# Four relus per step of the mixing stage handed from ScalarE to VectorE

## The chip, the core and the metric

The kernel runs on one core of one Trainium2 chip. The metric is the device time of one execution in microseconds; the time before is the median of three runs. The engines of the core, as the profile names them: PE is TensorE's matmuls and PEld its weight loads, DVE is VectorE, ACT is ScalarE, POOL is GpSimd, SP issues most DMAs. Each engine works through its own queue in order, and waits for others by semaphores.

## The reference

A block in three parts: three state-space layers, a complex diagonal recurrence over a layer norm, and a mixture of 32 experts of which each token takes one.

```python
def reference(x, ...):
    h = _L0_tok_ref(x, ...)                       # three state-space layers, halved twice in length
    h = h + _L0_attn_ref(_layernorm(h), ...)      # B u, scan with Lambda_bar, C x, + D u
    h = h + _L0_ffn_ref(_layernorm(h), ...)

def _L0_ffn_ref(x, router_w, router_b, W1, b1, W2, b2):   # E = 32 experts, H = 16 hidden
    logits = xf @ router_w.T + router_b
    idx = jnp.argmax(logits, axis=-1)
    h = jax.nn.relu(jnp.einsum('nd,ndh->nh', xf, W1[idx]) + b1[idx])
    out = jax.nn.relu(jnp.einsum('nh,nhd->nd', h, W2[idx]) + b2[idx])
```

The input is 128 x 375 x 64, the result 128 x 93 x 64. The hidden layer of all experts is 32 x 16 = 512 rows, four tiles of 128; the tokens' unchosen experts are pushed to -1e30 before the relu, so that they come out as zero.

## The kernel before

The first 5.8 ms are the three layers. VectorE scans there (L930), GpSimd multiplies the inputs (L1137), ScalarE takes the exponentials (L716). The change doesn't touch them.

The mixing stage does the other two parts for 16 chunks of 372 columns. Rows are 128: 64 channels of two batches, so every chunk is two halves, b = 0 and b = 1. `mix_steps` runs 20 steps, i = 0 to 19: two and two written out, ten in a hardware loop (steps 4 to 13), six written out. In step i five chunks are in work, a stage apart, and each engine's `step` names them: a = i is normed and driven into the recurrence, y = i - 1 is scanned and brought out, b = i - 2 is normed again and routed, e = i - 3 goes through the experts, f = i - 4 is finished and stored. So step 3 is the first with e, step 4 the first with f; the last with a is step 15, with y 16, with b 17, with e 18.

Per engine, in the order of a step:
- PE: center for a and b (L553); `up` for expert tile k=0 of e (L611 and L617, into the banks `bank_h[0]`, which is in decay, and `bank_h[1]`, which is z_bank); the variances (L553); `open_o` (L553, into prep_bank, the expert output's accumulator); `down` k=0 (L631) and `up` k=1; `output` for y (L553, four instructions with u as operand); `drive` for a; `route` for b; `up` k=2; `open_y`; `down` k=1; `up` k=3; `down` k=2; `turn` (L601, transposes of the choice); `down` k=3. The four `up` of a chunk share one pair of banks, so each waits until the one before has been read.
- ACT: `copy_cold` (L872, L873), squares (L862), `rectify` k=0, the two inverse deviations (L866, L868), `rectify` k=1 to 3. A `rectify` is two relus with bias (L880), one per half, out of `bank_h[b]` into `hid[k % 2][b]`.
- DVE: `scans` (L1085, L1087), `turn_back` (L1093, L1094), `finish` of f (L1100), `scale` for a and b (L1042), the addition of y's output (L1046), four `products` for a (L1053), `pick` for b (L1069 to L1079).
- POOL: `turn` of y (L1153, L1154, then the sums L1159 and L1162, which need DVE's turn_back), `turn_drive` of a (L1168, L1170).

`hid`, `u` and `hT` are one storage for the profile: a relu reads as hT<-decay,u or hT<-z_bank,u. The semaphores that matter: B["hid"] counts up's tiles, B["relu"] the relus read by `up` and `down`, B["down"] frees `hid`, A["qdve"] hands turn_back to POOL, A["turned"] hands POOL's sums to `output`. `open_o` of chunk e waits for B["fin"] of the chunk before it, which is f of the same step, since both use prep_bank:

```python
            def open_o(c):
                pe.wait_ge(B["copied"], 2 * c + 2)
                if not known_below(c, 1):
                    pe.wait_ge(B["fin"], c)
```

Of the kernel before, what the change touches and what calls it, by code (L numbers as in the profile page):

```python
# [6 lines left out]
ALU = mybir.AluOpType  # L7
ACT = mybir.ActivationFunctionType
# [33 lines left out]
TILES = E_FFN // EXP_PER_TILE  # L42
# [11 lines left out]
def known_below(n, limit):  # L54

    return isinstance(n, int) and n < limit


def tower(nc, io, hs, out_dram, n_batch):
# [13 lines left out]
    with ctx:  # L73
# [6 lines left out]
        def sem(name):  # L80
            return ctx.enter_context(nc.semaphore(name))
# [62 lines left out]
        ones_row, b1, eps = u[1][0:1, 1600:1728], u[1][:, 1728:1728 + TILES], u[1][:, 1740:1741]  # L144
        q = [u[2][:, i * W0:(i + 1) * W0] for i in range(4)]
        re, nim = [u[2][:, i * W0:(i + 1) * W0] for i in (4, 5)]
        fin, hot = u[2][:, 6 * W0:7 * W0], u[2][:, 7 * W0:8 * W0]
# [7 lines left out]
        hid = [[hT[1][:, (2 * i + b) * W0:(2 * i + b + 1) * W0] for b in range(2)] for i in range(2)]  # L155
# [5 lines left out]
        bank_h = [db[2][:, BANK:BANK + W0], zb[:, 0:W0]]  # L161
# [14 lines left out]
        m_set = sem("m_consts_set")  # L176
        A = {n: sem("A_" + n) for n in ("xc", "sq", "var", "log", "rstd", "u", "bu", "du", "prod", "w", "z", "qpool", "qdve", "turned", "y", "h")}
        B = {n: sem("B_" + n) for n in ("xc", "sq", "var", "log", "rstd", "u", "logits", "pick", "coldT", "copied",
                                        "hid", "relu", "down", "fin", "out")}
        N_WEIGHTS, N_SMALL = 15, 2  # L180

        def chunk(c):
            return h3[:, bass.ds(c * W0, W0)]

        def stage(i, lag):

            if isinstance(i, int) and not 0 <= i - lag < chunks:
                return None
            return i - lag
# [193 lines left out]
        def _(pe):  # L383
# [221 lines left out]
            def up(half, c, k):  # L605

                if k or not known_below(c, 1):
                    pe.wait_ge(B["relu"], 2 * (TILES * c + k))
                for b in range(2):
                    at = slice(D * b, D * (b + 1))  # L610
                    nc.tensor.matmul(bank_h[b], w1[at, P * k:P * (k + 1)], uB[half][at, :],  # L611
                                     start=True, stop=False, tile_position=(D * b, 0))
                if k == 0:
                    pe.wait_ge(B["copied"], 2 * c + 2)
                for b in range(2):
                    at = slice(D * b, D * b + E_FFN)
                    last = nc.tensor.matmul(bank_h[b], expand[at, k, :], coldT[at, :],  # L617
                                            start=False, stop=True, tile_position=(D * b, 0))
                last.then_inc(B["hid"], 1)
# [6 lines left out]

            def down(c, k):

                pe.wait_ge(B["relu"], 2 * (TILES * c + k + 1))
                for b in range(2):  # L630
                    last = nc.tensor.matmul(bank_o[D * b:D * (b + 1), :], w2[:, D * k:D * (k + 1)], hid[k % 2][b],  # L631
                                            start=False, stop=(k == TILES - 1), tile_position=(0, D * b))
                last.then_inc(B["down"], 1)

            def step(half, i):
# [6 lines left out]
                if e is not None:  # L642
                    up(other, e, 0)
# [46 lines left out]
        def _(act):  # L690
# [184 lines left out]
            def rectify(c, k):  # L875
                act.wait_ge(B["hid"], TILES * c + k + 1)
                if k >= 2 or not known_below(c, 1):
                    act.wait_ge(B["down"], TILES * c + k - 1)
                for b in range(2):
                    nc.scalar.activation(hid[k % 2][b], bank_h[b], ACT.Relu, bias=b1[:, k:k + 1]).then_inc(B["relu"], 1)  # L880

            def step(half, i):
                a, _, b, e = [stage(i, lag) for lag in range(4)]
# [29 lines left out]
        def _(dve):  # L913
# [44 lines left out]
            ts, stt = nc.vector.tensor_scalar, nc.vector.scalar_tensor_tensor  # L958
# [70 lines left out]
            def seqs(t):  # L1029
                return t.rearrange("p (s t) -> p s t", s=SEQS)  # L1030

            def every(t):
                return t.unsqueeze(1).broadcast_to([P, SEQS, T3])

            def scale(s, c, xc, rs, out):
                dve.wait_ge(s["rstd"], c + 1)
                if s is A:
                    if not known_below(c, 1):
                        dve.wait_ge(A["du"], c)
                elif not known_below(c, 2):  # L1040
                    dve.wait_ge(B["hid"], TILES * (c - 1))
                tt(out, xc, rs, ALU.mult).then_inc(s["u"], 1)  # L1042

            def add_output(c):
                dve.wait_ge(A["y"], c + 1)
                tt(chunk(c), chunk(c), bank_y, ALU.add).then_inc(A["h"], 1)  # L1046

            def products(c):
                dve.wait_ge(A["bu"], c + 1)
                if not known_below(c, 1):  # L1050
                    dve.wait_ge(A["w"], 2 * c)
                for i, (bank, table) in enumerate(((bank_v, T1R), (bank_x, T1I), (bank_v, T1I), (bank_x, T1R))):
                    tt(seqs(pr[i]), seqs(bank), every(table), ALU.mult).then_inc(A["prod"], 1)  # L1053

            def pick(c):

                dve.wait_ge(B["logits"], c + 1)
                if not known_below(c, 1):
                    dve.wait_ge(B["coldT"], c)
                shape = [TOK, 2 * NTOK, E_FFN]  # L1060

                def e3(t):
                    return t[0:TOK, 0:2 * NTOK * E_FFN].rearrange("p (j e) -> p j e", e=E_FFN)

                def over(t):
                    return t[0:TOK, :].unsqueeze(2).broadcast_to(shape)

                n = 5 * c
                nc.vector.reduce_max(top[0:TOK, :], e3(bank_xb), mybir.AxisListType.X).then_inc(B["pick"], 1)  # L1069
                dve.wait_ge(B["pick"], n + 1)  # L1070
                tt(e3(eq), e3(bank_xb), over(top), ALU.is_equal).then_inc(B["pick"], 1)
                dve.wait_ge(B["pick"], n + 2)
                tt(score[0:TOK, :], eq[0:TOK, :], rev[0:TOK, :], ALU.mult).then_inc(B["pick"], 1)
                dve.wait_ge(B["pick"], n + 3)
                nc.vector.reduce_max(top2[0:TOK, :], e3(score), mybir.AxisListType.X).then_inc(B["pick"], 1)
                dve.wait_ge(B["pick"], n + 4)

                cold = cold_rows[0:TOK, :].rearrange("p (j e) -> p j e", e=D)[:, :, 0:E_FFN]
                tt(cold, e3(score), over(top2), ALU.not_equal).then_inc(B["pick"], 1)  # L1079

            def scans(c):
                if not known_below(c, 1):
                    dve.wait_ge(A["qpool"], 2 * c)
                dve.wait_ge(A["w"], 2 * c + 1)
                nc.vector.tensor_tensor_scan(zr, DEC, wr, 0.0, ALU.mult, ALU.add).then_inc(A["z"], 1)  # L1085
                dve.wait_ge(A["w"], 2 * c + 2)
                nc.vector.tensor_tensor_scan(zi, DEC, wi, 0.0, ALU.mult, ALU.add).then_inc(A["z"], 1)  # L1087

            def turn_back(c):
                dve.wait_ge(A["z"], 2 * c + 2)  # L1090
                if not known_below(c, 1):
                    dve.wait_ge(A["turned"], 2 * c)
                tt(seqs(q[2]), seqs(zi), every(NSIN), ALU.mult).then_inc(A["qdve"], 1)  # L1093
                tt(seqs(q[3]), seqs(zi), every(COS), ALU.mult).then_inc(A["qdve"], 1)  # L1094

            def finish(c):
                dve.wait_ge(B["down"], TILES * c + TILES)
                if not known_below(c, 1):
                    dve.wait_ge(B["out"], 16 * c)
                stt(fin, bank_o, 0.0, chunk(c), ALU.max, ALU.add).then_inc(B["fin"], 1)  # L1100

            def step(half, i):
                a, y, b, _, f = [stage(i, lag) for lag in range(5)]
                if y is not None:
                    scans(y)
                    turn_back(y)
                if f is not None:
                    finish(f)
                if a is not None:
                    scale(A, a, bank_x, rsA, uA)  # L1110
                if b is not None:
                    scale(B, b, bank_xb[:, 0:W0], rsB, uB[half])
                if y is not None:
                    add_output(y)
                if a is not None:
                    products(a)
                if b is not None:
                    pick(b)

            dve.wait_ge(m_load, 16 * N_WEIGHTS)  # L1120
            mix_steps(dve, FIRST_STEPS, step)
# [139 lines left out]
def build(nc, io, out_dram, n_batch):  # L1261
    pairs = n_batch // 2
    hs = [nc.dram_tensor(f"h_after{l}", (P, pairs * LENGTHS[min(l + 1, LAYERS - 1)]), FP32, kind="Internal").ap()
          for l in range(LAYERS)]
    tower(nc, io, hs, out_dram, n_batch)
# [15 lines left out]
```

## Time and profile before

| | before |
|---|---|
| median of 3 runs | 6117.61 us (6111.73 to 6119.73) |
| profiled execution, its time | 6110.93 us |
| profiled execution, its span | 6109.1 us |
| mean granted TensorE clock | 0.983 |
| busy over the span: PE, DVE, ACT, POOL | 77%, 97%, 82%, 96% |

The span runs from the first instruction to the last; the profiled execution's time has 1.8 us around it. The shares are those of the layers, which fill 95% of the span. The mixing stage is seen in a stretch of its own: steps 4 to 15 run from 5875.05 to 6070.24 us. The columns of a stretch are, after its two ends, its length, then for PE, PEld, DVE, ACT and POOL the busy us and the count of instructions, then the granted clock as a share of full speed, the DMA share and GB/s. In a timeline, "x4" is a merged group of four, and the bracket gives how long the engine sat idle before it and who released it. A matmul's length is modelled and overlaps the next one's start; two `up` matmuls side by side run at once in halves of the array.

### The profile page before, as it was taken

Reading aid. Unit: us, or ns where it says so; the run is one execution under the profiler, and the core shown is the slowest. Engines: PE = TensorE matmul, PEld = TensorE weight load, DVE = VectorE, ACT = ScalarE, POOL = GpSimd, SP = SyncE. Lnnn points to the kernel's source line nnn. Section 1 sums busy time; section 2 is a strip of 40 time slices with the busy share of each in tenths; the row PEclk is TensorE's granted clock in tenths of the full one; section 3 lists DMA queues with packets and bytes.
Section 4 is the critical chain, followed back from the end, with each engine's and each line's share of the span. In section 5 each row is a group of like instructions: output and inputs, shape, how many; then the busy total and the mean of one; then the engine's idle time right before and its main releaser. Section 6 shows DMA issues by size and latency. Waiting matters only on the chain.

```text
span 6109.1 us, 97254 instructions
## 1 busy us (share of the span) xinstructions
PE 4718.7 (77%) x36042; PEld 1952.1 (32%) x36042; DVE 5950.6 (97%) x4016; ACT 5013.3 (82%) x10247; POOL 5888.7 (96%) x996
## 2 busy tenths in 40 slices
PE   6777777777777777777777777777777777777789
PEld 2333333333333333333333333333333333333234
DVE  8999999999999999999999999999999999999965
ACT  7888888888888888888888888888888888888844
POOL 8999999999999999999999999999999999999943
PEclk9999999999999999999999999999999999999999
DMA  7888888888888888888888888888888888888710
GB/s 256 270 269 270 268 269 269 269 269 269 268 268 269 265 272 269 268 270 268 265 267 268 271 269 267 268 269 269 269 270 269 269 269 270 270 270 271 259 42 14
DMA packets 562034, 1565.40 MB, mean 256 GB/s; under 512 B 172129, under 2 KB 320546, under 8 KB 561442
## 3 DMA queue, kind: packets, MB, share of 16 engines
q1 hardware_dynamic: 561570, 1559.30, 78.5%
q8 instruction: 281, 4.60, 0.3%
q14 instruction: 183, 1.50, 0.1%
HBM read 1468.37 MB, written 90.59 MB: 255 GB/s over the span
## 4 chain that ended last, share of the span: by engine, by line
DVE 45%; POOL 44%; issue 6%; PE 5%; ACT 0%; DMA 0%; SPq 0%; ACTq 0%; DVEq 0%; POOLq 0%
DVE hT L930 45%; POOL u L1137 44%; PE decay L553 2%; PE decay L611 1%; PE prep_bank L631 1%; DVE dx L941 0%; PE z_bank L418 0%; PE decay L617 0%; PE decay L400 0%; PE prep_bank L553 0%; PE prep_bank L506 0%; PE decay L601 0%; DMA u<-dx_rows 0%; ACT hT L880 0%; DVE hT L1053 0%
## 5 line engine op out<-in xcount | busy, mean ns | idle before, releaser
L1137 POOL TENSOR_TENSOR u<-u,Bt 128x2976 f32<-128x2976 f32 x896 | 5781.5, 6511 | 28.0 <-DMA u<-dx_rows 27.9
L930 DVE TENSOR_TENSOR_SCAN hT<-decay,u 128x744 f32<-128x744 f32 x3584 | 5740.5, 1681 | 17.4 <-POOL u L1137 12.5
L716 ACT ACTIVATE decay<-decay,a_neg 128x371 f32<-128x371 f32 (+2 forms) x7168 | 3604.1, 545 | 585.6 <-PE decay L400 555.5
L400 PE MATMUL decay<-stk,spread 96*128 96x371 bf16 (+2 forms) x7168 | 1788.4, 332 | 1353.9 <-DVE hT L930 1211.5
L418 PE MATMUL z_bank<-hT,Cst 128*32 128x256 f32 x21472 | 1468.5, 392 | 0.3 <-ACT z_sb L725 0.3
L400 PEld LDWEIGHTS decay<-stk,spread 96*128 96x128 bf16 x7168 | 416.2, 98 | 2852.2 <-DVE hT L930 2678.9
L725 ACT COPY z_sb<-z_bank 128x512 f32<-128x512 f32 x1342 | 790.9, 589 | 259.7 <-PE z_bank L418 259.5
L418 PEld LDWEIGHTS z_bank<-hT,Cst 128*32 128x32 f32 x21472 | 568.1, 111 | 672.3 <-issue 447.0
L428 PE MATMUL z_bank<-stk,spread 96*128 96x372 bf16 x1677 | 355.9, 321 | 0.0
L506 PE MATMUL prep_bank<-tmap,yT 64*128 64x32 f32 (+3 forms) x1344 | 215.3, 281 | 0.6 <-DMA yT<-y_rows 0.6
L506 PEld LDWEIGHTS prep_bank<-tmap,yT 64*128 64x128 f32 x1344 | 177.3, 190 | 110.5 <-issue 109.2
L428 PEld LDWEIGHTS z_bank<-stk,spread 96*128 96x128 bf16 x1677 | 163.4, 97 | 103.3 <-issue 1.1
L479 PE MATMUL prep_bank<-delta,eye 128*128 128x372 f32 x448 | 186.0, 497 | 2.2 <-DVE dx L941 1.7
L1168 POOL TENSOR_TENSOR hT<-hT 128x372 f32<-128x372 f32 x16 | 15.5, 971 | 126.4 <-DVE hT L1053 126.4
L754 ACT ACTIVATE Cst<-prep_bank,own_batch 128x384 f32<-128x384 f32 x224 | 132.3, 591 | 0.0
L880 ACT ACTIVATE hT<-decay,u 128x372 f32<-128x372 f32 x64 | 36.5, 570 | 110.6 <-PE z_bank L617 110.6
L451 PE MATMUL prep_bank<-xT,w_dt_rows 128*128 128x372 f32 x224 | 90.9, 487 | 9.1 <-DMA eye<-in_ident 6.5
L481 PE MATMUL prep_bank<-parts,neg_eye 128*128 128x372 bf16 x336 | 92.2, 329 | 0.0
L778 ACT COPY delta<-prep_bank 128x372 f32<-128x372 f32 x112 | 52.5, 469 | 47.3 <-PE prep_bank L469 47.3
L461 PE MATMUL prep_bank<-t_w,eye 128*128 128x372 f32 x224 | 89.7, 482 | 1.8 <-ACT t_w L763 1.8
L464 PE MATMUL prep_bank<-t_one,eye 128*128 128x372 f32 x224 | 89.7, 481 | 0.0
L468 PE MATMUL prep_bank<-t_ln,eye 128*128 128x372 f32 x224 | 89.5, 481 | 0.0
(140 smaller groups left out, 2533.7 us busy)
## 6 DMA issues: line engine op xcount, KB each, us to landing
u<-dx_rows SPq DMA_DIRECT2D x3584, 372.0 KB, 4.3
delta_parts<-parts SPq DMA_DIRECT2D x112, 279.0 KB, 6.5
stk<-delta_parts SPq DMA_DIRECT2D x112, 279.0 KB, 5.6
y_rows<-z_sb SPq DMA_DIRECT2D x1792, 12.0 KB
yT<-y_rows SPq DMA_DIRECT2D x112, 192.0 KB, 4.6
dx_rows<-dx SPq DMA_DIRECT2D x112, 186.0 KB, 2.8
xT<-in_x SPq DMA_DIRECT2D x64, 186.0 KB, 4.7
xP<-in_x SPq DMA_DIRECT2D x64, 186.0 KB, 4.7
```

The lines of the kernel that those rows point to most:

```text
L400: nc.tensor.matmul(slot[:, e, :, 1:], spread[0:PARTS * QR, TILES_G * q + er // TILES_G, :], src[:, er % TILES_G, :, 1:], start=True, stop= ...
L418: last = nc.tensor.matmul(bank[TB * 2 * g:TB * 2 * (g + 1), kk * EPT * TB:(kk + 1) * EPT * TB], Cst[buf][:, CG * (2 * i + kk) + g, :, :], ...
L428: nc.tensor.matmul(zb[:, 0:W0], spread[0:PARTS * QR, 0, :], stk[buf][0:PARTS * QR, 0, :], start=True, stop=True)
L479: nc.tensor.matmul(prep[:, 0:W0], eye[:, :], delta[:, :], start=True, stop=False)
L481: last = nc.tensor.matmul(prep[:, 0:W0], neg_eye[:, :], parts[:, j, :], start=False, stop=(j == i))
L506: last = nc.tensor.matmul(prep[:, k * w:k * w + m], yT[:, k, :], tmap[:, base:base + m], start=False, stop=(k == KB - 1))
L553: return nc.tensor.matmul(dst, wt, src, start=start, stop=stop)
L716: last = nc.scalar.activation(bank, bank, ACT.Exp, scale=a_neg[:, l, c:c + 1])
L725: nc.scalar.copy(z_sb[buf][:, 2 * i:2 * i + 2, :, q * EPT:(q + 1) * EPT], src).then_inc(s_zev, 1)
L754: ins = nc.scalar.activation(Cst[buf][:, :, b, :], prep[:, 0:COLS_Z].rearrange("p (k t) -> p k t", t=TB), ACT.Identity, scale=own[:, b:b + 1])
L930: nc.vector.tensor_tensor_scan(hT[q % 2][:, i * PAIR:(i + 1) * PAIR], pair_slot(turn, p), u[c % RING][:, part * PAIR:(part + 1) * PAIR], 0 ...
L1137: tt(here, here, Bt[buf][:, :].unsqueeze(1).broadcast_to([P, 2 * HALVES * CHUNK, W0]), ALU.mult).then_inc(s_u, 1)
```

## The change

A new `rectify` in VectorE's queue takes the half b = 1: one tensor_scalar, add the bias and take the maximum with zero, from `bank_h[1]` into `hid[k % 2][1]`. It waits for the same B["hid"] and B["down"] as ScalarE's, and counts a semaphore of its own, B["reluv"]. ScalarE's `rectify` keeps the half b = 0. `up` and `down` wait for both counts. In VectorE's step the four calls stand behind the scans (k=0), behind the scales (k=1), behind the products (k=2) and behind pick (k=3).

```diff
--- before.py
+++ after.py
@@ -176,7 +176,7 @@
         m_set = sem("m_consts_set")
         A = {n: sem("A_" + n) for n in ("xc", "sq", "var", "log", "rstd", "u", "bu", "du", "prod", "w", "z", "qpool", "qdve", "turned", "y", "h")}
         B = {n: sem("B_" + n) for n in ("xc", "sq", "var", "log", "rstd", "u", "logits", "pick", "coldT", "copied",
-                                        "hid", "relu", "down", "fin", "out")}
+                                        "hid", "relu", "reluv", "down", "fin", "out")}
         N_WEIGHTS, N_SMALL = 15, 2
 
         def chunk(c):
@@ -605,7 +605,8 @@
             def up(half, c, k):
 
                 if k or not known_below(c, 1):
-                    pe.wait_ge(B["relu"], 2 * (TILES * c + k))
+                    pe.wait_ge(B["relu"], TILES * c + k)
+                    pe.wait_ge(B["reluv"], TILES * c + k)
                 for b in range(2):
                     at = slice(D * b, D * (b + 1))
                     nc.tensor.matmul(bank_h[b], w1[at, P * k:P * (k + 1)], uB[half][at, :],
@@ -626,7 +627,8 @@
 
             def down(c, k):
 
-                pe.wait_ge(B["relu"], 2 * (TILES * c + k + 1))
+                pe.wait_ge(B["relu"], TILES * c + k + 1)
+                pe.wait_ge(B["reluv"], TILES * c + k + 1)
                 for b in range(2):
                     last = nc.tensor.matmul(bank_o[D * b:D * (b + 1), :], w2[:, D * k:D * (k + 1)], hid[k % 2][b],
                                             start=False, stop=(k == TILES - 1), tile_position=(0, D * b))
@@ -876,8 +878,7 @@
                 act.wait_ge(B["hid"], TILES * c + k + 1)
                 if k >= 2 or not known_below(c, 1):
                     act.wait_ge(B["down"], TILES * c + k - 1)
-                for b in range(2):
-                    nc.scalar.activation(hid[k % 2][b], bank_h[b], ACT.Relu, bias=b1[:, k:k + 1]).then_inc(B["relu"], 1)
+                nc.scalar.activation(hid[k % 2][0], bank_h[0], ACT.Relu, bias=b1[:, k:k + 1]).then_inc(B["relu"], 1)
 
             def step(half, i):
                 a, _, b, e = [stage(i, lag) for lag in range(4)]
@@ -1093,6 +1094,13 @@
                 tt(seqs(q[2]), seqs(zi), every(NSIN), ALU.mult).then_inc(A["qdve"], 1)
                 tt(seqs(q[3]), seqs(zi), every(COS), ALU.mult).then_inc(A["qdve"], 1)
 
+            def rectify(c, k):
+
+                dve.wait_ge(B["hid"], TILES * c + k + 1)
+                if k >= 2 or not known_below(c, 1):
+                    dve.wait_ge(B["down"], TILES * c + k - 1)
+                ts(hid[k % 2][1], bank_h[1], b1[:, k:k + 1], 0.0, ALU.add, ALU.max).then_inc(B["reluv"], 1)
+
             def finish(c):
                 dve.wait_ge(B["down"], TILES * c + TILES)
                 if not known_below(c, 1):
@@ -1100,9 +1108,12 @@
                 stt(fin, bank_o, 0.0, chunk(c), ALU.max, ALU.add).then_inc(B["fin"], 1)
 
             def step(half, i):
-                a, y, b, _, f = [stage(i, lag) for lag in range(5)]
+                a, y, b, e, f = [stage(i, lag) for lag in range(5)]
                 if y is not None:
                     scans(y)
+                if e is not None:
+                    rectify(e, 0)
+                if y is not None:
                     turn_back(y)
                 if f is not None:
                     finish(f)
@@ -1110,12 +1121,18 @@
                     scale(A, a, bank_x, rsA, uA)
                 if b is not None:
                     scale(B, b, bank_xb[:, 0:W0], rsB, uB[half])
+                if e is not None:
+                    rectify(e, 1)
                 if y is not None:
                     add_output(y)
                 if a is not None:
                     products(a)
+                if e is not None:
+                    rectify(e, 2)
                 if b is not None:
                     pick(b)
+                if e is not None:
+                    rectify(e, 3)
 
             dve.wait_ge(m_load, 16 * N_WEIGHTS)
             mix_steps(dve, FIRST_STEPS, step)
```

VectorE's queue at the opening of a step, here step 14, the first behind the loop. Before: scans, turn_back, finish, the scales.

```order
L1085 SCALAR_TENSOR_TENSOR hT<-tables,hT 128x372 [waits A_w,A_qpool]
L1087 SCALAR_TENSOR_TENSOR hT<-tables,hT 128x372 [waits A_w]
L1093 TENSOR_TENSOR u<-hT,tables 128x372 [waits A_turned,A_z]
L1094 TENSOR_TENSOR u<-hT,tables 128x372
L1100 SCALAR_TENSOR_TENSOR u<-prep_bank,z_sb 128x372 [waits B_out,B_down]
L1042 TENSOR_TENSOR hT<-decay,hT 128x372 [waits A_du,A_rstd]
L1042 TENSOR_TENSOR hT<-decay,hT 128x372 [waits B_hid,B_rstd]
```

After, from the scans to the relu of k=1 (z_bank is `bank_h[1]`):

```order
L1086 SCALAR_TENSOR_TENSOR hT<-tables,hT 128x372 [waits A_w,A_qpool]
L1088 SCALAR_TENSOR_TENSOR hT<-tables,hT 128x372 [waits A_w]
L1102 TENSOR_SCALAR hT<-z_bank,u 128x372 [waits B_down,B_hid]
L1094 TENSOR_TENSOR u<-hT,tables 128x372 [waits A_turned,A_z]
L1095 TENSOR_TENSOR u<-hT,tables 128x372
L1108 SCALAR_TENSOR_TENSOR u<-prep_bank,z_sb 128x372 [waits B_out,B_down]
L1043 TENSOR_TENSOR hT<-decay,hT 128x372 [waits A_du,A_rstd]
L1043 TENSOR_TENSOR hT<-decay,hT 128x372 [waits B_hid,B_rstd]
L1102 TENSOR_SCALAR hT<-z_bank,u 128x372 [waits B_down,B_hid]
```

The relu of k=0, which waits for TensorE's tile of this step, now stands ahead of turn_back and of finish.

ScalarE's queue in the same step, from the first square on, before:

```order
L862 ACTIVATE hT<-decay 128x372 [waits A_xc]
L862 ACTIVATE hT<-decay 128x372 [waits B_xc]
L880 ACTIVATE hT<-decay,u 128x372 [waits B_down,B_hid]
L880 ACTIVATE hT<-z_bank,u 128x372
L866 ACTIVATE hT<-decay,u 128x372 [waits A_var]
L868 ACTIVATE hT<-hT 128x372 [waits A_log]
L866 ACTIVATE hT<-decay,u 128x372 [waits B_var]
L868 ACTIVATE hT<-hT 128x372 [waits B_log]
L880 ACTIVATE hT<-decay,u 128x372 [waits B_down,B_hid]
L880 ACTIVATE hT<-z_bank,u 128x372
```

After:

```order
L864 ACTIVATE hT<-decay 128x372 [waits A_xc]
L864 ACTIVATE hT<-decay 128x372 [waits B_xc]
L881 ACTIVATE hT<-decay,u 128x372 [waits B_down,B_hid]
L868 ACTIVATE hT<-decay,u 128x372 [waits A_var]
L870 ACTIVATE hT<-hT 128x372 [waits A_log]
L868 ACTIVATE hT<-decay,u 128x372 [waits B_var]
L870 ACTIVATE hT<-hT 128x372 [waits B_log]
L881 ACTIVATE hT<-decay,u 128x372 [waits B_down,B_hid] x3
```

Each pair of relus has become one; its waits are the same.

## Rows read from the trace of the kernel before

**Rows 1.** Busy time by stretch, steps 4 to 15; columns as in the line of engines above.

```profile
5875.05:6070.24 195.19, 195.19 (x853) 85.97 (x853) 118.56 (x205) 94.58 (x193) 80.28 (x73) 1.00 0.03 12
```

**Rows 2.** Timeline, opening of one steady step; start, length, engine, line, instruction, operands.

```profile
5971.57 1.07 DVE L1093 TENSOR_TENSOR u<-hT,tables 128x372 f32<-128x372 f32 x1
...
5972.56 1.25 DVE L1094 TENSOR_TENSOR u<-hT,tables 128x372 f32<-128x372 f32 x1
...
5973.74 0.53 DVE L1100 SCALAR_TENSOR_TENSOR u<-prep_bank,z_sb 128x372 f32<-128x372 f32 x1
...
5974.61 0.96 POOL L1162 TENSOR_TENSOR u<-u 128x372 f32<-128x372 f32 x1
...
5975.30 0.57 ACT L880 ACTIVATE hT<-decay,u 128x372 f32<-128x372 f32 x1 [0.69 <-PE z_bank L617]
...
5976.46 0.79 PE L553 MATMUL prep_bank<-u 128*128 128x372 f32 x2
...
5979.05 1.52 PE L553 MATMUL decay<-u 128*128 128x372 f32 x4
```

**Rows 3.** Timeline, end of the step before that one, all engines.

```profile
5967.49 0.35 DVE L1069 TENSOR_REDUCE u<-decay 124x6 f32<-124x192 f32 x1
...
5967.98 0.57 ACT L880 ACTIVATE hT<-decay,u 128x372 f32<-128x372 f32 x1 [4.06 <-PE z_bank L617]
...
5969.29 0.36 DVE L1079 TENSOR_TENSOR u<-u 124x192 f32<-124x192 f32 x1
...
5970.67 0.57 ACT L880 ACTIVATE hT<-decay,u 128x372 f32<-128x372 f32 x1 [1.65 <-PE z_bank L617]
...
5971.33 0.54 PE L601 MATMUL decay<-eye,u 124*128 124x124 f32 x3
...
5971.80 0.85 PE L631 MATMUL prep_bank<-hT,u 128*64 128x372 f32 x4
```

**Rows 4.** Timeline, VectorE instructions from which prices are taken.

```profile
21.35 0.41 DVE L1020 TENSOR_SCALAR tables<-tables,z_sb 128x368 f32<-128x368 f32 x1
...
5965.67 1.90 DVE L1053 TENSOR_TENSOR hT<-decay,tables 128x372 f32<-128x372 f32 x4 [0.69 <-PE decay L553]
...
5968.27 0.60 DVE L1073 TENSOR_TENSOR u<-u 124x192 f32<-124x192 f32 x1
...
6079.04 0.36 DVE L1073 TENSOR_TENSOR u<-u 124x192 f32<-124x192 f32 x1
```

**Rows 5.** Timeline, steps 16 to 18, TensorE and ScalarE.

```profile
6072.20 0.57 ACT L880 ACTIVATE hT<-decay,u 128x372 f32<-128x372 f32 x1 [0.61 <-PE z_bank L617]
...
6072.81 0.79 PE L553 MATMUL prep_bank<-u 128*128 128x372 f32 x2
...
6080.43 0.58 PE L611 MATMUL decay<-hT,u 64*128 64x372 f32 x1 [0.35 <-ACT hT L880]
...
6096.44 0.89 PE L553 MATMUL prep_bank<-u 128*128 128x372 f32 x2
...
6096.55 0.57 ACT L880 ACTIVATE hT<-decay,u 128x372 f32<-128x372 f32 x1 [1.02 <-PE z_bank L617]
...
6097.02 0.56 ACT L880 ACTIVATE hT<-z_bank,u 128x372 f32<-128x372 f32 x1
...
6097.63 0.84 PE L631 MATMUL prep_bank<-hT,u 128*64 128x372 f32 x4 [0.30 <-ACT hT L880]
...
6100.69 0.58 PE L611 MATMUL decay<-hT,u 64*128 64x372 f32 x1 [1.12 <-ACT hT L880]
```

**Rows 6.** Timeline and busy time by stretch, TensorE in steps 2 and 3.

```profile
5849.94 1.52 PE L553 MATMUL decay<-u 128*128 128x372 f32 x4 [1.75 <-POOL u L1162]
...
5856.84 0.54 PE L601 MATMUL decay<-eye,u 124*128 124x124 f32 x3 [2.14 <-DVE u L1079]
5857.21 2.22 PE L553 MATMUL decay<-z_sb,u 128*128 128x372 f32 x4
...
5858.00:5860.00 2.00, 2.00 (x5) 0.83 (x5) 1.97 (x3) 1.19 (x3) 2.00 (x2) 0.50 0.00 0
```

## The prediction

> **What bounds the kernel now.** I read the slices of the span first, then the granted clock, then the mixing stage alone. The change touches only that stage: twenty steps behind the last scan of the three state-space layers, about the last 290 of 6109 us. In busy time by stretch, TensorE is busy for all of the 195.19 us of steps 4 to 15, at the full granted clock [rows 1]; that is 16.27 us a step. VectorE has work for 118.56 us of them and ScalarE for 94.58 us. So what ends last in a steady step is TensorE's own queue, and no engine that gets rid of work there gives time back. A step can only grow, if TensorE is made to wait. Only in the last three steps, where few chunks are left in flight, does TensorE wait for ScalarE's two relus [rows 5].
>
> So the question is which VectorE results TensorE needs, and when. I put the timeline of one steady step next to VectorE's order of work. VectorE runs ahead: it turns the chunk back (L1093, L1094) at 5971.57 and 5972.56, finishes the oldest chunk (L1100) at 5973.74, and is done with that at 5974.27, while the first hidden tile of this step is there only at 5975.30, when ScalarE's first relu starts [rows 2]. TensorE opens the output bank (L553, prep_bank) at 5976.46; open_o waits for this very finish, because the bank still holds the oldest chunk. The slack is 2.2 us.
>
> **Part by part.** *ScalarE loses one relu of two, four times a step.* In steps 4 to 15 this is worth nothing: TensorE has no gap behind it [rows 1].
>
> *VectorE gains four instructions a step*, some 2.2 us on 9.9 of 16.27 us: no bound as a sum. What matters is the place. The first one (k=0) stands between the scans and turn_back, and VectorE takes its queue in order. Behind it are queued: both turn_back products (GpSimd waits for them, and TensorE's output for GpSimd), then finish (TensorE's open_o waits for it, and behind open_o all the rest of the step). In the order before, none of these waited for the hidden tile; now all do. The walk, from the hidden tile at 5975.30 [rows 2]:
> - relu, then the first product 0.50 later. Four PSUM-read products in a row take 1.90 us, the last 0.54 of it, so 0.45 from start to start [rows 4]; I add 0.05 for the column of biases.
> - first product to second 0.50. It is 0.99 in the trace [rows 2], but there GpSimd works beside it. Now GpSimd has long done its own two products when VectorE comes, and sits waiting. A product with both operands in SBUF takes 0.60 beside GpSimd and 0.36 alone [rows 4]; so I take the uncontended pace, 0.50, with 0.99 as the upper end.
> - second product to finish 1.10. In the trace it is 1.18 [rows 2]. GpSimd's sum is released by the first product, so it again runs beside the second one. Lower end 0.50, if it did not matter.
> - finish 0.53 [rows 2], hand-over to TensorE 0.05 (a relu that starts at 6097.02 and lasts 0.56 releases a matmul at 6097.63 [rows 5]).
>
> That is 2.68 us: open_o at 5977.98 and not at 5976.46, **1.52 us later per step**. TensorE idles for it, and everything behind it moves along. Twelve steps: 18.2 us. In step 3 there is no finish, so it is free of this.
>
> *The other three relus* I cost at nothing, and name the cover. k=1 runs between scale and the output's addition, where VectorE idles anyway. k=2 is put ahead of pick. Pick starts at 5967.49 but the hidden tile is there only at 5967.98; so it waits 0.49 and then takes 0.50 for the relu, and ends at 5970.65 plus 0.05 instead of 5969.65. TensorE's transposes of its result start at 5971.33 [rows 3]: 0.6 us are left. k=3 comes behind it, at its hidden tile of 5970.67, and ends at about 5971.25, and TensorE's use of it is at 5971.80 [rows 3]. This slack moves along with the step.
>
> *A rule weighed.* The relu reads PSUM. The one instruction of its kind and width in the trace reads SBUF and takes 0.41 [rows 4], while reads from PSUM with the same columns go at 0.54. I take the PSUM price. The Trainium skill, VectorE: DVE Perf Modes, section Why PSUM operands drop a tier, says that fp32 with a PSUM operand stays at the plain rate, which speaks for the same. With 0.41's pace each step would lose 1.4 us, and the sum would be some 2 us lower.
>
> *The two added waits of TensorE* (reluv beside relu) sit on the same matmul instruction; the instruction count of its queue is the same, and I cost them at nothing.
>
> *Last steps.* Step 16 still has turn_back, but no new chunk, so open_o stood only 0.61 behind the hidden tile [rows 5]: 2.68 - 0.61 = 2.07 later; the relu gap of 0.35 [rows 5] goes: +1.7. Step 17 has only finish behind the relu: 0.50 + 0.53 + 0.05 = 1.08, less the same 0.61, +0.47; its gap of 0.35 (as at 6080.43) goes: +0.1. Step 18: hidden tile at 6096.55, so open_o at 6097.63 and not 6096.44, but its down had waited until 6097.63 for the second relu, and now follows 0.72 after open_o, at 6098.35: +0.7. Behind it the gap of 1.12 shrinks by the 0.47 between the two relus' starts, and two gaps of 0.35 go: -1.2. Together -0.5.
>
> **Sum:** 18.2 + 1.7 + 0.1 - 0.5 = +19.6 us on the profiled execution of 6110.93, so 6130.5. The median of the runs shown is 6117.61, so the forecast is **6137.2 us**, 0.32% slower. About 0.2%, 12 us, is what a measurement can tell from no change here.
>
> **Rivals.**
> - *The port is free (ends on the other side).* If turn_back's second product goes at 0.50 too, open_o is late by 0.92 a step: 12 x 0.92 + 1.1 + 0.1 - 0.5 = +11.7, 6129.3, within 0.2%. It decides at 0.54 for that product's pace. For: the shares of contention are read from one row pair. Against: 1.25 us for this very instruction when GpSimd runs [rows 2], and the sum on GpSimd is released just as it starts. Chance 0.12.
> - *The clock falls.* An idle TensorE may get the low clock. After 1.75 us of idle the four matmuls took 1.52; after 2.14 us four took 2.22, at a granted clock of 0.50, that is 1.2 GHz [rows 6]. My 1.52 us lies below the first. If it falls in every step, it adds 0.70 for four matmuls, and I estimate twice that, 1.4, for the whole stretch: 12 x 1.4 = 17, 6154. It is at hand if the first product too is held up (0.99): then the idle is 2.0 and the sum without any clock effect +26. Chance 0.14 for both, from 6143 to 6157.
> - *The finish is not what binds.* If open_o had another cover, the next that is late would be the output's wait for GpSimd's last sum: it ended at 5975.57 against 5979.05 [rows 2], and the walk puts it at about 5978.3. Then only the last steps' gaps count, some -2 us: 6115.5. Against: the wait is in the code, and nothing else holds finish back. Chance 0.06.
> - *More waits in a chain.* If pick ends over 0.6 us later than I say, the transposes and with them the end of every step come late; each 0.1 us over it costs 1.2 us. Chance 0.05.
>
> **How the numbers follow.** Forecast 0.63. Range: from the free port to the fallen clock, 6127 to 6157; what is left out is the case that nothing binds and half of the long chain, under 0.1, plus the scatter of the runs. Slower by over 0.2%: the forecast, the clock and the chain, 0.81. Within 0.2%: free port and no binding, less a little, 0.17. Faster by over 0.2% would need 12 us, and the gaps behind relus hold under 3 us in all: 0.02.
>
> **What would show it.** Right: in steps 4 to 15 a step takes about 17.8 us; TensorE has one idle of about 1.5 us before open_o, released by VectorE's finish; VectorE's longest wait is for the hidden tile, between the scans and turn_back; the first product of turn_back is short (about 0.55) and the second long (over 1). The last step is shorter. Wrong: steps of 16.3 us; an idle ahead of the transposes or the output instead; a granted clock under 1.00 in these steps.

## The result: 14 us slower, and the profile after

| | before | changed |
|---|---|---|
| median of 20 runs | 6113.14 us (6107.73 to 6119.73) | 6127.59 us (6120.2 to 6131.05) |
| ratio, 95% interval | | 1.0024 (1.0018 to 1.003) |
| profiled execution, span | 6109.1 us | 6123.7 us |

The change costs 14.5 us by the medians, 0.24%. The forecast was 6137.2, +19.6 us on a median of 6117.61 from three runs; over twenty runs the kernel before has 6113.14. So of the 9.6 us between forecast and result, 4.5 are the base and 5.1 are the cost.

The two profiled spans differ by 14.6 us. By stretch, with the columns as ahead of the prediction; first the changed kernel, steps 4 to 15 and the rest of the span behind them:

```profile
5875.72:6083.25 207.53, 198.08 (x855) 84.88 (x853) 127.12 (x253) 73.89 (x145) 75.80 (x73) 1.00 0.03 11
6083.25:6123.70 40.45, 33.49 (x162) 12.65 (x160) 15.26 (x32) 11.88 (x23) 4.02 (x4) 1.00 0.05 19
```

and the same two stretches of the kernel before:

```profile
5874.97:6070.17 195.20, 195.20 (x854) 85.97 (x852) 118.58 (x205) 94.59 (x193) 80.29 (x73) 1.00 0.03 12
6070.17:6109.10 38.93, 33.10 (x162) 12.66 (x160) 8.29 (x18) 17.17 (x35) 2.76 (x3) 1.00 0.06 20
```

The twelve steady steps take 207.53 us instead of 195.20, +12.3, and the last three with what follows +1.5. The remaining 0.7 us up to the span's 14.6 lie ahead of step 4: the layers ended 3.7 us earlier in this execution and steps 0 to 3 took 4.5 us longer. That part does not follow the edit, as the nine traces show below under "Steps 0 to 3". In the steady stretch TensorE is no longer busy throughout: 198.08 of 207.53 us.

Timeline of one steady step's opening in the changed kernel, all engines (it corresponds to [rows 2]; L1102 is VectorE's relu, L1108 finish):

```profile
5962.26 1.52 PE L553 MATMUL decay<-z_sb,u 128*128 x4
...
5964.99 0.57 ACT L881 ACTIVATE hT<-decay,u 128x372 f32<-128x372 f32 x1 [0.69 <-PE z_bank L618]
5965.00 0.60 DVE L1102 TENSOR_SCALAR hT<-z_bank,u 128x372 f32<-128x372 f32 x1 [2.38 <-PE z_bank L618]
5965.52 0.54 DVE L1094 TENSOR_TENSOR u<-hT,tables 128x372 f32<-128x372 f32 x1
...
5965.98 0.54 DVE L1095 TENSOR_TENSOR u<-hT,tables 128x372 f32<-128x372 f32 x1
5966.19 1.17 POOL L1176 TENSOR_TENSOR u<-u 128x372 f32<-128x372 f32 x1 [1.99 <-DVE u L1094]
...
5966.44 0.54 DVE L1108 SCALAR_TENSOR_TENSOR u<-prep_bank,z_sb 128x372 f32<-128x372 f32 x1
...
5967.12 0.86 PE L553 MATMUL prep_bank<-u 128*128 128x372 f32 x2 [0.80 <-DVE u L1108]
...
5967.32 0.97 POOL L1179 TENSOR_TENSOR u<-u 128x372 f32<-128x372 f32 x1
...
5979.57 1.52 PE L553 MATMUL decay<-z_sb,u 128*128 x4
```

VectorE stands idle for 2.38 us ahead of the relu of k=0, with turn_back and finish queued behind it. Then relu, two products and finish run in one go, and TensorE's open_o is released by finish, after 0.80 us of idle. From the hidden tile (5964.99) to open_o it is 2.13 us; in the kernel before 1.16 [rows 2]. The step is 17.31 us instead of 16.27.

### The profile page after: what moved, and what is told of

It reads as the page before. It is cut to its first block, busy times and chain, and to the rows that moved or that the text cites. A ratio compares the mean times of both kernels' runs of the same rounds, so it can differ in the third digit from the quotient of the medians.

```text
span 6123.7 us, 97478 instructions
## 1 busy us (share of the span) xinstructions
PE 4705.0 (77%) x36042; PEld 1942.5 (32%) x36042; DVE 5967.1 (97%) x4080; ACT 4995.7 (82%) x10183; POOL 5883.6 (96%) x996
## 4 chain that ended last, share of the span: by engine, by line
POOL 88%; issue 7%; PE 4%; DVE 1%; DMA 0%; SPq 0%; ACT 0%; DVEq 0%; POOLq 0%; ACTq 0%
POOL u L1154 88%; PE decay L553 2%; PE decay L612 1%; PE prep_bank L633 1%; PE decay L618 0%; PE prep_bank L553 0%; DVE hT L931 0%; PE decay L601 0%; DVE u L1108 0%; DMA u<-dx_rows 0%; DVE u L1095 0%; DVE u L1094 0%; DVE hT L1054 0%; DVE hT L1086 0%; POOL u L1170 0%
## 5 line engine op out<-in xcount | busy, mean ns | idle before, releaser
L1102 DVE TENSOR_SCALAR hT<-z_bank,u 128x372 f32<-128x372 f32 x64 | 38.7, 605 | 79.4 <-PE z_bank L618 79.4
```

## The experiments

The base of every edit is the changed kernel. Lengths of steps are from start to start of the centering matmuls (L553, decay<-z_sb).

**Finish ahead of the relu.**

```diff
                 if y is not None:
                     scans(y)
+                if f is not None:
+                    finish(f)
                 if e is not None:
                     rectify(e, 0)
                 if y is not None:
                     turn_back(y)
-                if f is not None:
-                    finish(f)
```

> The changed kernel with one swap in VectorE's step: finish stands ahead of the relu of k=0, turn_back behind it. Theory (the whole cost is finish held back by the wait for the hidden tile): open_o finds its bank free, steps 4 to 15 take 16.27 us again, TensorE has no idle before open_o; GpSimd's last sum comes about 3.3 us behind the hidden tile and TensorE's output 3.75 behind it, so that turn_back's delay stays hidden. Against the kernel before: 0 to -2 us, ratio 0.9997 to 1.0000. Rival 1 (turn_back's delay counts too): an idle ahead of the output, steps of 16.5 to 17 us, +3 to +9 us. Rival 2 (it is VectorE's extra load, or the second wait on TensorE's matmuls): steps stay at 17.3 us, ratio 1.002.

Measured: 6114.19 us, ratio 0.9999 (0.999 to 1.0009), as the theory has it and neither rival. Steps 4 to 15 and the rest, by stretch:

```profile
5880.38:6075.58 195.20, 195.20 (x854) 85.85 (x852) 128.50 (x253) 73.91 (x145) 75.84 (x73) 1.00 0.03 12
6075.58:6112.60 37.02, 33.10 (x162) 12.85 (x160) 15.45 (x32) 11.87 (x23) 4.02 (x4) 1.00 0.06 21
```

VectorE has a little more to do than in the changed kernel (128.50 us), TensorE's matmuls still wait for two semaphores, and the twelve steps are back at 195.20. So neither the load nor the second wait costs anything. And turn_back, which still stands behind the relu, is hidden, with little to spare; the timeline of one step:

```profile
5980.73 0.60 DVE L1102 TENSOR_SCALAR hT<-z_bank,u 128x372 f32<-128x372 f32 x1 [1.88 <-PE z_bank L618]
...
5981.87 0.79 PE L553 MATMUL prep_bank<-u 128*128 128x372 f32 x2
...
5983.05 0.97 POOL L1179 TENSOR_TENSOR u<-u 128x372 f32<-128x372 f32 x1
...
5984.45 1.52 PE L553 MATMUL decay<-u 128*128 128x372 f32 x4
```

GpSimd's last sum ends at 5984.02 and TensorE's output starts at 5984.45, unhindered: 0.43 us are left. The last steps are 1.9 us shorter than before the change (37.02 against 38.93). That is the change's whole gain. It is read from one trace of each kernel, and too small to be seen in the comparison of runs.

**Relu behind turn_back and finish.**

```diff
-                if e is not None:
-                    rectify(e, 0)
                 if y is not None:
                     turn_back(y)
                 if f is not None:
                     finish(f)
+                if e is not None:
+                    rectify(e, 0)
```

> The changed kernel with the relu of k=0 behind turn_back and finish instead of ahead of them; all four relus stay on VectorE. Theory: nothing that TensorE or GpSimd needs is queued behind the hidden tile any more; steps 4 to 15 take 16.27 us, the last three steps are some 2 us shorter than before. Ratio to the kernel before 0.9995 to 1.0000. Rival (load or second wait): steps of 17.3 us, ratio 1.002.

Measured: 6113.69 us, ratio 1.0 (0.9991 to 1.0009).

```profile
5878.42:6073.62 195.20, 195.20 (x855) 85.86 (x853) 142.95 (x253) 73.91 (x145) 80.31 (x73) 1.00 0.03 12
6073.62:6111.20 37.58, 33.26 (x162) 12.77 (x160) 16.70 (x32) 11.87 (x23) 4.40 (x4) 1.00 0.06 21
```

All four relus are on VectorE, which is now busy for 142.95 us, more than in any other of these kernels, and nothing is lost. A surprise is that figure: the same 253 instructions take 14.5 us more than with finish alone moved. The timeline shows where: turn_back meets GpSimd's products again, as it did before the change.

```profile
5976.42 1.07 DVE L1094 TENSOR_TENSOR u<-hT,tables 128x372 f32<-128x372 f32 x1
5977.05 1.21 POOL L1171 TENSOR_TENSOR u<-hT,tables 128x372 f32<-128x372 f32 x1
5977.41 1.25 DVE L1095 TENSOR_TENSOR u<-hT,tables 128x372 f32<-128x372 f32 x1
```

**Only k=0 given back to ScalarE**, and **only k=0 on VectorE.** KS stands here for the tuple that says which relus of the half b = 1 are VectorE's: (1, 2, 3) in the first kernel, (0,) in the second. The counts that TensorE waits for in `up` and `down` follow from it and are left out here. The first piece of the diff is ScalarE's rectify, the second VectorE's.

```diff
             def rectify(c, k):
...
-                nc.scalar.activation(hid[k % 2][0], bank_h[0], ACT.Relu, bias=b1[:, k:k + 1]).then_inc(B["relu"], 1)
+                for b in range(1 if k in KS else 2):
+                    nc.scalar.activation(hid[k % 2][b], bank_h[b], ACT.Relu, bias=b1[:, k:k + 1]).then_inc(B["relu"], 1)
...
             def rectify(c, k):
+                if k not in KS:
+                    return
```

> Of the change only k=1, 2 and 3 are left on VectorE; both relus of k=0 are ScalarE's again. Theory: steps of 16.27 us, the last steps about 1.5 us shorter, ratio 0.9996 to 1.0000. Rival (each of the four relus bears its share): three quarters of the cost stay, +10 us, steps of 17.0 us.

Measured: 6113.94 us, ratio 0.9998 (0.9989 to 1.0007).

> Of the change only k=0 is on VectorE, still ahead of turn_back and finish; ScalarE takes both relus of k=1, 2 and 3. Theory: steps of 17.3 us as in the changed kernel, +12.5 us for steps 4 to 15, and +3 in the last steps, whose gaps behind the relus stay: ratio 1.0020 to 1.0030. Rival (shares): a quarter of the cost, +3.6 us, ratio 1.0006.

Measured: 6133.92 us, ratio 1.0028 (1.0013 to 1.0044). Steps 4 to 15 of the one and of the other:

```profile
5881.78:6076.98 195.20, 195.20 (x854) 85.86 (x853) 136.82 (x241) 78.11 (x157) 80.30 (x73) 1.00 0.03 12
```

```profile
5881.32:6088.83 207.51, 198.06 (x854) 84.86 (x852) 108.80 (x216) 90.50 (x181) 75.86 (x73) 1.00 0.03 11
```

One relu of the four bears the whole cost: without it 195.20 us, with it alone 207.51, as in the changed kernel. The last steps are 37.9 us in the first and 42.2 in the second, 1.7 more than in the changed kernel; that is what k=1 to 3 give back there.

**GpSimd kept busy.** It gets one product more per step, whose result is not used. GpSimd's `step` passes e along, which is left out here.

```diff
-            def turn(c):
+            def turn(c, e):
...
                 tt(seqs(q[1]), seqs(zr), every(NSIN), ALU.mult).then_inc(A["qpool"], 1)
+                if e is not None:
+                    pool.wait_ge(B["hid"], TILES * e + 1)
+                    tt(hT[1][:, 8 * W0:10 * W0], hT[1][:, 4 * W0:6 * W0], hT[1][:, 6 * W0:8 * W0], ALU.mult)
```

> The changed kernel, and GpSimd gets one product more per step: 128x744, both operands in SBUF, result unused, released by the hidden tile of k=0, so that it starts with VectorE's relu of k=0 and lasts some 1.75 us (372 columns take 0.97). It is there to hold whatever VectorE and GpSimd share while turn_back's first product wants to start, 0.52 us behind the hidden tile. Theory A (taken in turns: a two-operand product waits until the other engine's instruction has ended, then runs its 0.4 us): the relu, which reads PSUM, stays at 0.60; the first product lasts about 1.6 us and ends 0.4 us behind GpSimd's; the second one is 0.54 as in the changed kernel; open_o comes 1.1 us later than there, steps of 18.3 us, +13 us on the changed kernel, ratio to the kernel before 1.0045. Theory B (shared rate, both slowed while both run): the first product lasts about 0.95 us, steps of 17.7 us, ratio 1.0032. Theory C (nothing shared): 0.54 and 17.3 us.

Measured: 6152.5 us, ratio 1.0055 (1.0038 to 1.0071). Timeline of one step, VectorE and GpSimd (L1174 is the added product), then TensorE:

```profile
6008.60 1.75 POOL L1174 TENSOR_TENSOR hT<-hT 128x744 f32<-128x744 f32 x1 [0.75 <-PE z_bank L618]
...
6008.65 0.60 DVE L1102 TENSOR_SCALAR hT<-z_bank,u 128x372 f32<-128x372 f32 x1 [2.37 <-PE z_bank L618]
6009.17 1.59 DVE L1094 TENSOR_TENSOR u<-hT,tables 128x372 f32<-128x372 f32 x1
6010.68 0.53 DVE L1095 TENSOR_TENSOR u<-hT,tables 128x372 f32<-128x372 f32 x1
...
6011.82 0.86 PE L553 MATMUL prep_bank<-u 128*128 128x372 f32 x2 [1.85 <-DVE u L1108]
```

The added product ends at 6010.35, VectorE's first product at 6010.76, 0.41 us behind it. Its 1.59 us are what theory A gave (1.6), and neither B's 0.95 nor C's 0.54; the ratio fits A's 1.0045 too, and B's 1.0032 lies below the interval. The relu beside it, which reads PSUM, is untouched at 0.60. So an instruction of VectorE with both tensor operands in SBUF waits here until GpSimd's instruction has ended, and then needs its 0.4 us. The Trainium skill, GPSIMD Engine Reference, section 8. Key points, says that GpSimd shares its SBUF interfaces with VectorE and contends with VectorE instructions that have two SBUF inputs, and the trace agrees (1.59 us against 0.54). That the wait lasts for the whole of GpSimd's instruction is read from these rows.

The steps, though, are 18.36 us only in eight of twelve cases. Four took 19.9. A step of each kind:

```profile
6005.91:6024.27 18.36, 16.50 (x73) 7.07 (x71) 11.54 (x22) 6.15 (x13) 8.06 (x8) 1.00 0.03 10
6024.27:6044.18 19.91, 18.05 (x73) 7.64 (x71) 11.54 (x22) 6.14 (x13) 8.06 (x8) 0.91 0.03 10
```

In the long one the granted clock is 0.91 in the mean, and TensorE's own work has grown by 1.55 us. It had idled 1.85 to 1.87 us ahead of open_o in all twelve. This count is of one execution, and the longest of the four: 6170.15 us, the others 6146.66 to 6154.76; some 17 us of it lie ahead of the mixing stage, which began at 5836.93 here and at 5819.82 in the kernel before.

**Finish behind both scales**, and **behind the first scale only**. The diff of the first, and then of the second:

```diff
                 if y is not None:
                     turn_back(y)
-                if f is not None:
-                    finish(f)
                 if a is not None:
                     scale(A, a, bank_x, rsA, uA)
                 if b is not None:
                     scale(B, b, bank_xb[:, 0:W0], rsB, uB[half])
+                if f is not None:
+                    finish(f)
```

```diff
-                if f is not None:
-                    finish(f)
                 if a is not None:
                     scale(A, a, bank_x, rsA, uA)
+                if f is not None:
+                    finish(f)
                 if b is not None:
                     scale(B, b, bank_xb[:, 0:W0], rsB, uB[half])
```

> The changed kernel with finish moved behind the two scales, which wait for ScalarE until 2.9 us behind the hidden tile. Theory (open_o follows finish): open_o starts 4.1 us behind the hidden tile instead of 2.13, TensorE's idle grows from 0.8 to 2.8 us, steps of 19.3 us: +24 us on the changed kernel, ratio to the kernel before 1.006 to 1.0065 at full granted clock. Rival (the clock falls behind an idle of this length, as in steps 2 and 3): a granted clock of 0.50 for part of every step, steps of 20 us and more, ratio above 1.0080.

Measured: 6174.63 us, ratio 1.0095 (1.0078 to 1.0112): the rival, the falling clock. Open_o and the down behind it, from TensorE's timeline, and the clock in one step and in 2 us of it:

```profile
6007.04 1.07 PE L553 MATMUL prep_bank<-u 128*128 128x372 f32 x2 [2.71 <-DVE u L1108]
6008.04 1.51 PE L633 MATMUL prep_bank<-hT,u 128*64 128x372 f32 x4
```

```profile
6000.28:6021.08 20.80, 18.09 (x74) 7.38 (x72) 10.66 (x22) 6.15 (x13) 6.29 (x7) 0.92 0.02 9
...
6008.00:6010.00 2.00, 2.00 (x7) 0.80 (x8) 0.00 (x0) 0.00 (x0) 0.00 (x0) 0.50 0.22 80
```

After 2.71 us of idle the clock is at 0.50 of full speed, 1.2 GHz, for a while; four matmuls of down take 1.51 us instead of 0.85. Twelve steps take 250.65 us, 20.9 each, where the idle alone would give 19.2.

> The changed kernel with finish behind the first of the two scales, which waits for ScalarE until 1.9 us behind the hidden tile. Finish then ends 2.9 us and open_o starts 3.0 us behind it, so that TensorE idles about 1.65 us in each of steps 4 to 15: close to the 1.52 us that the prediction took for its own case, and between the 0.8 us of the changed kernel (granted clock 1.00 throughout) and the 1.86 us at which 4 of 12 steps ran at a lower clock for a while. Theory A (the prediction's: no loss of clock below 1.75 us): all steps 18.15 us, +22.5 us on the kernel before for steps 4 to 15, ratio 1.004. Theory B (an idle of this length already costs the clock in some steps): single steps 1.5 us longer, as in the run with GpSimd kept busy.

Measured: 6139.95 us, ratio 1.0036 (1.0022 to 1.0049). TensorE idled 1.70 or 1.71 us ahead of open_o in each of the twelve steps, and all of them took 18.21 or 18.22 us. No step lost its clock:

```profile
5880.70:6099.23 218.53, 198.07 (x854) 84.87 (x852) 128.03 (x253) 73.81 (x145) 75.59 (x73) 1.00 0.03 11
```

That is theory A's outcome. It does not show that 1.75 us is a bound, as the traces of steps 0 to 3 below make plain.

The five lengths of idle side by side, all from steps 4 to 15. Each row is one profiled execution, and not all were taken on the same chip:

| kernel | idle before open_o | step | steps with a lower clock |
|---|---|---|---|
| finish ahead of the relu | 0 | 16.27 | 0 of 12 |
| changed kernel | 0.80 (0.71 in the last two) | 17.31 (17.22) | 0 of 12 |
| finish behind the first scale | 1.71 | 18.21 | 0 of 12 |
| GpSimd kept busy | 1.86 | 18.36, or 19.9 | 4 of 12 |
| finish behind both scales | 2.71 | 19.2 once, 20.8 nine times, 22.2 twice | 11 of 12 |

**Steps 0 to 3.** Steps 0 to 2 hold no relu yet, and step 3 the first four. Still the four steps together took

| before | changed | finish first | relu last | k=0 on ScalarE | only k=0 | GpSimd busy | behind both scales | behind the first |
|---|---|---|---|---|---|---|---|---|
| 55.15 | 59.61 | 57.65 | 57.14 | 59.62 | 55.16 | 55.70 | 57.49 | 57.38 |

The sums of the kernel before and of the one with only k=0 moved are alike, and so are those of the changed kernel and the one without k=0. So they don't follow the edit. The changed kernel and the kernel before differ in how long TensorE ran at the lower clock:

```profile
5816.11:5875.72 59.61, 48.10 (x186) 22.46 (x186) 31.84 (x53) 15.51 (x31) 21.95 (x21) 0.80 0.13 45
```

```profile
5819.82:5874.97 55.15, 43.66 (x186) 20.47 (x186) 32.67 (x51) 17.08 (x35) 23.88 (x22) 0.88 0.15 51
```

The difference is all in PE busy, 4.4 us, at a mean granted clock of 0.80 against 0.88. It arises in steps 2 and 3. In step 2 TensorE idles twice, ahead of the output and ahead of the transposes. In the kernel before these idles were 1.75 and 2.14 us; only around the second did the clock fall, to 0.50 from 5858 to 5860 [rows 6], and from 5862 on it was 1.00 again. In the changed kernel they were 2.22 and 2.14; the clock fell at both, and the second time it stayed low for at least 10 us:

```profile
5854.00:5864.00 10.00, 9.22 (x19) 4.16 (x19) 4.41 (x8) 4.51 (x9) 4.39 (x4) 0.50 0.00 1
```

In the kernel with only k=0 on VectorE the same two idles were 2.27 and 2.14 us, and the clock did not fall at all:

```profile
5857.89 1.52 PE L553 MATMUL decay<-u 128*128 128x372 f32 x4 [2.27 <-POOL u L1182]
...
5864.78 0.54 PE L601 MATMUL decay<-eye,u 124*128 124x124 f32 x3 [2.14 <-DVE u L1081]
```

```profile
5855.00:5869.00 14.00, 9.60 (x38) 4.96 (x38) 9.57 (x18) 4.81 (x10) 7.14 (x8) 1.00 0.10 28
```

So the length of an idle alone does not tell whether the clock falls.

## Why the prediction was right, and where a size was off

- *The number.* The result lies in the range, but only 0.6 us above its lower end of 6127, since the base came down as well. Taken from the base of three runs the range reached from +9.4 to +39.4 us, and the cost is 14.5. That is nearer to the rival of the free port (+11.7) than to the forecast (+19.6).
- *What bounds the step: right.* TensorE's queue; with open_o free, steps are 16.27 us whatever stands on VectorE.
- *The mechanism: right, and shown from both sides.* The k=0 relu holds finish, and finish holds open_o. Moving finish alone removes the whole 12.3 us; moving k=0 alone brings it all back.
- *The size per step: 1.04 us, not 1.52.* The term that failed is "second product to finish 1.10". It measured 0.46 (5965.98 to 5966.44). The premise was right, that GpSimd's sum is released by the first product and runs beside the second. The conclusion was not: the sum is released when the first product has ended, and by then the second one, which starts 0.46 behind the first, is under way. The sum waited instead (1.17 us, against 0.97 for the next one). I had carried over 1.18 from [rows 2] and misread what was running there. It was not the sum but GpSimd's second product, under way before VectorE's second product came at 5972.56; the sum started only at 5973.37:

```profile
5972.19 1.22 POOL L1154 TENSOR_TENSOR u<-hT,tables 128x372 f32<-128x372 f32 x1
...
5973.37 1.27 POOL L1159 TENSOR_TENSOR u<-u 128x372 f32<-128x372 f32 x1
```

  The two other steps of the walk, relu 0.52 and first product 0.46, were near their 0.50; the first product did find GpSimd idle.
- *Two smaller terms were too low.* The hand-over to TensorE: finish ends at 5966.98, open_o starts at 5967.12, 0.14 instead of 0.05; and from open_o to the next matmul it is 0.79 instead of 0.72. Together +0.16. The walk with all of these is 0.52 + 0.46 + 0.46 + 0.54 + 0.14 = 2.12, less 1.16, plus 0.07: 1.03 of the 1.04.
- *The rival "the port is free" named the right outcome for the wrong reason.* It gave 0.92 a step, +11.7 us. What the two engines share is not free: GpSimd's sum paid 0.20 us for it. The order in which two instructions come decides who waits, and here it favours VectorE.
- *The relu's price.* 0.60 us, 0.52 from start to start, was well taken from the rows on PSUM reads; the SBUF row of 0.41 would have been wrong. No row stood behind the 0.05 for the column of biases; 0.52 against 0.46 for the product behind it makes it 0.06. The "1.4 us" that each step would lose at 0.41's pace is a slip: 0.54 less 0.41 is 0.13 a step, and some 1.6 us over the twelve.
- *The other three relus at nothing: right.* Steps of 16.27 us with all three of them on VectorE. Pick did slide, and its cover held: it ends at 5977.42 and the transposes start at 5978.33, 0.9 us where 0.6 was forecast.
- *The last steps: the sum right, its parts not.* +1.3 was forecast and +1.5 measured. Step 16 grew by 1.26 us (14.63 against 13.37) and not by 1.7, and what follows it grew by 0.26 where it should have shrunk by 0.4. That the two errors largely cancel is luck. With the k=0 part removed the last steps are a gain of 1.9.
- *The clock: no fall, as forecast, but on a weak bound.* "No fall up to 1.75 us" was read from a single idle. In steps 4 to 15, idles of 1.71 us cost no clock in twelve cases, and idles of 1.86 did in four of twelve; but in step 2 of the kernel with only k=0, 2.27 and 2.14 us cost none. An idle of 1.52 us itself was not run; its neighbours of 0.80 and 1.71 cost nothing in these steps.
- *The base.* Three runs put the median 4.5 us above that of twenty.

## What to carry to other kernels

Before an instruction is slipped into another engine's queue, write down what stands behind it there and who waits for that; the load it adds can be harmless while its wait is not. Put the instruction with the latest input behind those whose results are awaited, and the same work is free: here 14 us hang on the order of two lines. And when a duration is taken over from a trace, ask which engine was there first: a VectorE instruction that waited in one order may be the one that is waited for in another.

## What the runs showed of the hardware

VectorE's two-operand SBUF instructions and GpSimd's take turns by whole instructions, in both directions. One VectorE product of 372 columns took 0.54 us alone, 1.07 and 1.25 behind GpSimd's products of the same size, and 1.59 behind a GpSimd product of 744 columns, always ending about 0.4 us behind the other's end; a GpSimd sum released while VectorE's product was under way took 1.17 us instead of 0.97.

Idles of TensorE of about 2 us can cost the clock in this kernel, but their length alone does not decide. In steps 4 to 15, one profiled execution each, 1.71 us of idle in every step of 18.2 cost nothing, 1.86 in a step of 18.4 cost 1.55 us in four of twelve steps, and 2.71 in a step of 19.2 cost 1.6 us in nine of twelve and 3 us in two. Yet in step 2 idles of 2.27 and 2.14 us left the clock at 1.00 in one execution, while 2.22 and 2.14 brought 0.50 in another. What decides it is open, and with it the difference of up to 4.5 us between executions in steps 0 to 3.
